# Moving the row scatters of a mixture-of-experts decoder layer to other attention heads

## What is computed

```python
x = x + attn(_layernorm(x), Wu, bu, Wv, bv, Wo, bo, zero, pos)   # gated Toeplitz mixer
x = x + xattn(_layernorm(x), ctx, Wq, Wk, Wv, Wo, proj)          # 16 heads, relu features, 77 context rows
x = x + ffn(_layernorm(x), router_w, w_gate, w_up, w_down)       # 8 experts, top 2

# ffn, cut
routing = softmax(xf @ router_w.T);  top_w, top_i = top_k(routing, 2);  top_w /= sum(top_w)
h = silu(xf @ w_gate[e].T) * (xf @ w_up[e].T);  y = h @ w_down[e].T
out = sum of y over the token's two experts, weighted by top_w
```

## Time and profile before

| what | value |
|---|---|
| median of 3 runs | 290.74 us (289.99 to 290.80) |
| the profiled execution | 288.63 us |
| its span on the core | 286.9 us |
| TensorE busy | 87% of the span |
| VectorE busy | 64% |
| GpSimd busy | 38% |
| attention, as the trace shows it | about 84 to 193 us |
| expert stage | about 193 to 274 us |

### The profile page before, as it was taken

How to read it: one execution, slowest core, us unless ns; L and a number is a source line. 1 busy time by engine, 2 the same in 40 slices (tenths; PEclk the granted TensorE clock), 3 DMA queues, 4 the chain that set the end, 5 groups by cost and what they waited for, 6 DMA issues and landing times.

```text
span 286.9 us, 5986 instructions
## 1 busy us (share of the span) xinstructions
PE 248.3 (87%) x1778; PEld 214.8 (75%) x1778; DVE 184.2 (64%) x737; ACT 158.8 (55%) x342; POOL 109.5 (38%) x163
## 2 busy tenths in 40 slices
PE   7899999999899999999999999887878797889700
PEld 3567776876689998999899988777778696789600
DVE  2777787959188879888888879897722122222216
ACT  3366564656767776777777766533334344445400
POOL 4288640702010001022423345745555555555520
PEclk9999999999999999999999999999979999999955
DMA  6979939999330000000000000348785967762147
GB/s 219 274 208 178 146 87 176 187 195 187 71 146 0 2 0 5 0 9 28 12 21 19 30 21 30 93 123 234 216 200 173 281 176 215 216 204 78 30 154 285
DMA packets 36255, 35.37 MB, mean 123 GB/s; under 512 B 3973, under 2 KB 27658, under 8 KB 36096
## 3 DMA queue, kind: packets, MB, share of 16 engines
q1 hardware_dynamic: 33520, 30.23, 44.4%
q0 software_dynamic: 2272, 4.24, 4.3%
q10 hardware_dynamic: 432, 0.52, 0.7%
HBM read 19.84 MB, written 14.32 MB: 119 GB/s over the span
## 4 chain that ended last, share of the span: by engine, by line
PE 67%; DVE 11%; DMA 7%; issue 5%; ACT 3%; POOL 2%; SPq 2%; another core or an unknown queue 1%; POOLq 0%; DVEq 0%; ACTq 0%
PE num L1581 14%; PE front L1694 12%; PE num L1704 7%; PE front L1513 5%; PE front L280 4%; PE num L1491 4%; PE front L282 4%; PE front L281 4%; DVE X L1084 3%; PE back L1455 2%; PE back L1402 2%; PE num L280 2%; DVE X L1393 2%; PE num L1686 2%; DMA wo_sb<-in_wo 2%
## 5 line engine op out<-in xcount | busy, mean ns | idle before, releaser
L1084 DVE SCALAR_TENSOR_TENSOR X<-num,rden,X 128x128 f32<-128x128 f32 x256 | 76.2, 343 | 4.5
L1581 PEld LDWEIGHTS num<-kvw_sb,q 128*128 128x128 f32 x512 | 65.8, 190 | 6.0 <-issue 1.4
L1581 PE MATMUL num<-kvw_sb,q 128*128 128x130 f32 x512 | 68.2, 276 | 1.2 <-DVE X L1084 1.2
L619 POOL DMA_INDIRECT dispatched<-rows,slot_i x32 | 31.4, 982 | 51.9 <-PE front L282 20.2
L663 POOL DMA_INDIRECT expert_out<-yo,xb x39 | 38.0, 974 | 33.1 <-ACT yo L826 17.1
L1366 DVE TENSOR_TENSOR hid<-front,silu_g 128x256 f32<-128x256 f32 x39 | 16.5, 423 | 51.1 <-ACT silu_g L822 41.0
L785 ACT ACTIVATE relu_z<-front 128x512 f32<-128x512 f32 x64 | 38.1, 596 | 19.4 <-PE front L282 18.9
L1694 PE MATMUL front<-xT,wgu_sb 128*128 128x128 f32 x312 | 43.0, 282 | 3.6 <-issue 2.0
L679 ACT ACTIVATE q<-relu_z 128x512 f32<-128x512 f32 x64 | 40.4, 632 | 5.9 <-PE num L1581 0.4
L1694 PEld LDWEIGHTS front<-xT,wgu_sb 128*128 128x128 f32 x312 | 39.0, 196 | 4.5 <-issue 4.5
L280 PE MATMUL front<-y2T_hi,feat_hi 128*128 128x512 f32 (+1 forms) x80 | 33.2, 415 | 0.3 <-ACT relu_z L785 0.3
(11 more groups left out here) (175 smaller groups left out, 366.9 us busy)
## 6 DMA issues: line engine op xcount, KB each, us to landing
wgu_sb<-in_wgu SPq DMA_DIRECT2D x39, 256.0 KB
dispatched<-pad_row SPq DMA_DIRECT2D x3, 2795.0 KB, 17.9
xb<-dispatched SPq DMA_DIRECT2D x39, 65.0 KB
y_back<-expert_out SPq DMA_DIRECT2D x4, 512.0 KB, 4.8
wd_sb<-in_wd SPq DMA_DIRECT2D x1, 1024.0 KB, 4.9
out<-X SPq DMA_DIRECT2D x4, 256.0 KB, 2.3
X<-in_x SPq DMA_DIRECT2D x3, 256.0 KB, 4.9
expert_out<-yo,xb POOLq DMA_INDIRECT x39, 3.0
```

The lines of the kernel that those rows point to most:

```text
L619: g.indirect_dma_start(out=xs, out_offset=bass.IndirectOffsetOnAxis(ap=slot_i[:, m % 2, t, k:k + 1], axis=0), in_=rows[:, m % 2, k, t, :], ...
L1084: ins = v.scalar_tensor_tensor(tile, banks[:, t // 2, t % 2, 0:P], rden[:, f % 2, t:t + 1], tile, ALU.mult, ALU.add)
L1581: last = nc.tensor.matmul(num[:, 2 * (h % 2) + t // 2, HA * (t % 2):HA * (t % 2 + 1)], q[:, h % 4, part], kvw_sb[:, n, HA * at:HA * (at + ...
```

## The change

Only the table of gates and one count change. Batch 0's scatters go four beside batch 1 and four beside batch 2 (two and six before); batch 1's go four beside batch 2 and four beside batch 3 (two and six before). Batch 2's eight have gates at half heads 13 to 27 of batch 3 (19 to 30 before), and those of job 3 at 29 to 35 (31 to 37 before). The norm of job 3 stands behind three scatters of batch 2 in GpSimd's program (four before).

```diff
-        SPREAD = {(1, 0): (26, 30), (2, 0): (2, 6, 10, 14, 18, 22), (2, 1): (26, 30), (3, 1): (1, 5, 9, 12, 15, 17),
-                  (3, 2): (19, 20, 22, 23, 25, 27, 28, 30), (3, 3): (31, 33, 35, 37)}
-        NORM_AT, HALF_NORM_AT = 2, 4
+        SPREAD = {(1, 0): (21, 24, 27, 30), (2, 0): (2, 6, 10, 14), (2, 1): (21, 24, 27, 30), (3, 1): (1, 4, 7, 10),
+                  (3, 2): (13, 15, 17, 19, 21, 23, 25, 27), (3, 3): (29, 31, 33, 35)}
+        NORM_AT, HALF_NORM_AT = 2, 3
```

## The result

The changed kernel takes 292.06 us (median of 20 runs, 290.53 to 294.6), the kernel before 289.88 us (median of 20 runs beside them, 286.17 to 291.75): 2.2 us more, where the forecast was 0 to +0.5. The ratio given with the result is 1.0129, 95% interval 1.0102 to 1.0156; the two medians alone make 1.0075. All ratios here leave out runs more than 1.5% above the fastest of the same kernel, taken as a slower state, which drops eight of the twenty runs before and none after, so that 1.0129 is likely too large. Both intervals lie above 1.003: **slower**, where the forecast was no change.

What follows compares the result with a forecast made beforehand. TensorE was taken as full, GpSimd not. Batches 0, 1 and job 3 cost nothing; batch 2's last scatter, 0.20 us later, gave +0.1 (0 to +0.5): 290.8 us from the median, own range 290.0 to 291.6, 8 in 10 289.3 to 292.1.

Steps and rivals of the forecast that it cites:

- Batches 0 and 1: Attention, scatters of batches 0 and 1: places or an unharmed norm decide, last scatters go earlier unawaited; cost nothing.
- The step that failed: Opening step: GpSimd is not full, so a scatter's 0.96 us costs only through what waits for it.
- the gate waits of 0.17 and 0.62 us: Batch 2's scatters behind the norm: idle above the 0.30 gap, counted as gains within 1.07 us together.
- A rule weighed: Bunched scatters beside VectorE: shared SBUF interfaces could stretch them; by the profile's durations the rule adds nothing.
- Job 3, "nothing": Job 3's four scatters: places come at 190.29 to 190.45, so they stay, first at 191.24; cost nothing.
- (a): Five scatters behind the norm, sharing DMA engines with weight loads, get longer; experts 1.4 us later, 292.1 us; chance 0.11.
- (b): Batch 2's scatters follow their gates, last one 3.1 us earlier, rows come early: 290.3 to 288.1 us; chance 0.07.
- (c): Expert stage: the lull at 209 to 210 with half clock goes (289.1 us) or a second appears (292.4); 0.08 each side.
- crowding loads: First silu at 196.94, 2.2 us late, perhaps from row and weight loads crowding together; used in rival (b).

Runs made afterwards that it cites:

- eight in a row: Kernel before, with all eight scatters of batch 1 at half head 21 of batch 2, ahead of the weight loads: 292.01 us, ratio 1.0167.
- the gates that let GpSimd pause: Changed kernel, with later gates for batch 2 (19 to 31) and job 3 (31 to 37), norm still behind three scatters: 287.42 us, ratio 1.0016.
- the part on batch 2 alone: Changed kernel with the old gates of batches 0 and 1 put back, keeping the edits of batch 2, job 3 and the norm: 291.96 us, ratio 1.0065.
- the row of four behind the norm: Changed kernel with job 3's norm behind four scatters of batch 2 instead of three: 290.92 us, ratio 1.0048.
- the second execution of the same kernel: The changed kernel timed and traced once more with no edit, against the kernel before: 291.94 us, ratio 1.0077.
- the run with the weight loads behind: Changed kernel with SyncE's weight loads of blocks 0 to 2 moved behind its wait for scatters and first two row loads: 289.75 us, ratio 1.0063.

## Why the prediction was wrong

**Right, by its steps.** Batches 0 and 1 cost nothing that can be measured (1.0016, 0.9987 to 1.0045, alone). Batch 2's first scatter at 177.25, for 177.16. The norm waits for the moments and starts at 181.76, for 181.66. Five in a row, the last at 188.39, for 188.28. SyncE's first row loads issue at 191.05, for 190.89. No scatter is longer than the prediction had it.

**The step that failed** stands at the very beginning: "a scatter's own 0.96 us costs nothing in itself; it can cost only through what waits for it". From it followed that five scatters in a row are worth what the last one's lateness is worth, +0.1 us. The runs showed a third way to pay: while GpSimd issues scatters without a pause, ScalarE and VectorE take up TensorE's finished results late. Nothing waits for the scatters, and the bill still comes: 2.20 and 1.62 us for ScalarE and 2.73 for VectorE in the row of five, and TensorE's idle 3.09 us with the half clock behind it. In the prediction's sum this term was missing, not mis-sized: it had +0.1 us, and the medians are 2.2 us apart. That 292.06 still lies inside the range of 8 in 10, at its very end (292.1), is owed to the room left for the rivals; the range of the forecast itself ended at 291.6. The prediction counted the gate waits of 0.17 and 0.62 us as gains from their removal. Together they kept the five from standing in one row; which of the two did it was not tested.

**"A rule weighed"** asked the right question of the wrong column. It compared durations, and these did not change: the 32 scatters after have a minimum of 956 and a median of 960 ns, the 958 of before and 2 more. The hold is in the idle time before instructions of other engines. The Trainium skill (GPSIMD Engine Reference, Key points) speaks of contention at shared SBUF interfaces; no stretched instruction shows that here, and ScalarE, which the rule does not name, is held as VectorE is. The weighted sums were no fair test of the rule either: num lies in PSUM, so only X and the small rden come from SBUF.

**Job 3, "nothing"**, fell with it. The four scatters were expected to stay because their places come at 190.29; the places came at 193.27, as VectorE was held.

**The rivals.** (a) had the place, the five scatters behind the norm, and came near the time: 292.1 us for 292.06 measured. It had the wrong mechanism, scatters that get longer, and none of the five took more than 1.09 us. That its price fits is chance: it puts the experts 1.4 us later, the profile has 4.37, less what the expert stage gave back. (b) did not happen. (c) happened in part: the half clock behind the lull at 209 went away, as one side of it said, while TensorE's idle time there stayed 2.1 us and moved to 210.7 to 214.2, and this came with a shift of 3 us and not of 0.2.

**What was there to be read.** Batch 2's own row of four before (177.16 to 181.91) shows a hold in ScalarE's timeline, for features that had ended at 181.70:

```profile
182.95 0.60 ACT L785 ACTIVATE relu_z<-front 128x512 f32<-128x512 f32 x1 [1.12 <-PE front L282]
```

And the chain of the kernel before carries the mark in the expert stage, where GpSimd's sends of outputs follow one another, with the silu that waited behind the second of them:

```profile
240.56 1.94 another core or an unknown queue
255.43 1.95 another core or an unknown queue
```

```profile
254.53 0.97 POOL L663 DMA_INDIRECT expert_out<-yo,xb  x1 [0.48 <-issue]
256.00 0.97 POOL L663 DMA_INDIRECT expert_out<-yo,xb  x1 [0.50 <-issue]
```

```profile
257.40 0.38 ACT L822 ACTIVATE silu_g<-front 128x256 f32<-128x256 f32 x1 [1.97 <-remote]
```

Here the gaps between the sends are 0.48 and 0.50 us, and the wait is there all the same: gaps of this size are no pause. On one core, with no other to signal to it, a row like "another core or an unknown queue" is a question that wants an answer before a schedule with denser scatters is priced. So was the silu that came 2.2 us late behind job 3's row of four, which the prediction put down to crowding loads.

**What stays open.** That rows without a pause bring the holds, and pauses take them away, is shown (eight in a row, the gates that let GpSimd pause, and the part on batch 2 alone). That TensorE's signals are what is held is the reading of these rows, and no experiment tried it by itself; what in the chip would hold them is not known. It was only seen that ScalarE's last hold ended 1.07 to 1.21 us behind the end of the last scatter in all rows of five and in the row of four behind the norm, and 1.68 behind the row of eight, and that in three of the five traces with a row of five another hold ended 0.35 to 0.39 us behind the start of the fourth scatter. Also open is how much weight loads lengthen a hold, why rows of four (batch 2's before, batch 1's after) cost little in time, and how the loss splits between waiting and clock, since the half clock lasted 6 us in one execution of the changed kernel and 3 us in the other.

## What to carry to other kernels

Read a row of indirect transfers on GpSimd as a load on everyone who waits for TensorE, even when nobody waits for the transfers: count how many go without a pause. Here gaps of 0.30 us, and of 0.48 and 0.50 between sends, were no pause; pauses of 0.81 and 0.94 us, never more than two scatters apart, were enough in the one schedule that tried them. A gate that seems to cost GpSimd idle time may be that pause; before removing it, look at the idle time of ScalarE and VectorE beside a dense row, not only at the durations. On a single core, take "remote" or "an unknown queue" in a chain as a finding in itself.

## What the runs showed of the hardware that was not expected

With indirect transfers 1.26 us apart on GpSimd (0.96 of work, 0.30 of gap), ScalarE and VectorE started on finished results of TensorE late: 1.86 us of idle in one place in a row of four, 2.20, 1.62 and 2.73 in a row of five, 1.74, 4.45, 3.68 and 1.53 in a row of eight, also with the DMA engines at a share of 0.20 or less. TensorE took VectorE's results in the middle of such a row at once (0.06 us behind their end). A memset of 0.11 us between the transfers changes nothing in it; idle gaps of 0.81 and 0.94 us do away with it. TensorE, once idle for 3.09 us behind such a hold, was granted 1.2 GHz for the next 6 us of full work (in the second execution of the same kernel, after 3.12 us, for some 3 us), and after 2.25 us of idle in the run with eight in a row it had the same clock from 162 to 168. After 1.57 us of idle in the run with the weight loads behind, it kept 2.4 GHz.
